# Token copies on one engine as 32-bit words, and a re-timed norm: one change to a fused group-norm and channel-attention kernel

## The reference

```python
g = x.reshape(B, 32, 6, H, W)                      # group norm: 32 groups of 6 channels
xn = (g - mean) / sqrt(var + 1e-5)
q, k, v = split(xn_tokens @ w_qkv)                 # 8 heads of 24 channels
q, k = q / |q|, k / |k| * temperature              # norms over all 2304 pixels
attn = softmax(k^T q)                              # 24 x 24 per head: attention over channels
out = x + from_tokens(attention(v, attn) @ w_out + b_out)
```

## Time and profile before

| | |
|---|---|
| median of three runs | 440.52 us (440.19 to 440.92) |
| the profiled execution | 436.02 us |
| its span, first to last instruction | 434.2 us |
| TensorE matmuls busy | 349.3 us, 80% |
| VectorE busy | 315.4 us, 73% |
| ScalarE busy | 247.4 us, 57% |
| GpSimd busy | 141.1 us, 33% |
| mean granted TensorE clock | 0.976 of full speed |
| DMA | 67.90 MB, 156 GB/s over the span |

### The profile page before, as it was taken

One profiled execution on the slowest core, in us unless ns is written; L12 is line 12 of the kernel. 1 busy time (PEld: TensorE's weight loads), 2 busy tenths in 40 slices (PEclk: granted clock), 3 DMA queues, 4 the chain that ended last, 5 costly groups with the idle time before them and its releaser, 6 DMA issues.

```text
span 434.2 us, 9296 instructions
## 1 busy us (share of the span) xinstructions
PE 349.3 (80%) x3724; PEld 238.5 (55%) x3724; DVE 315.4 (73%) x757; ACT 247.4 (57%) x360; POOL 141.1 (33%) x92
## 2 busy tenths in 40 slices
PE   0123863799988998899979997999799988996686
PEld 0022643585657565765667565756575657663443
DVE  4789932898589867897689758975897675446564
ACT  1072747881887368944986297719782788310200
POOL 0056425610571048302750075106710572001000
PEclk9999998799999999999999999999999999998699
DMA  8999300001894169605980399129921650053165
GB/s 296 286 298 249 74 2 0 2 2 75 253 324 118 53 191 323 200 2 153 335 276 3 127 283 327 30 79 292 302 95 72 194 154 20 33 188 109 51 195 190
DMA packets 30682, 67.90 MB, mean 156 GB/s; under 512 B 5360, under 2 KB 11824, under 8 KB 30640
## 3 DMA queue, kind: packets, MB, share of 16 engines
q1 hardware_dynamic: 30352, 66.86, 48.9%
q10 hardware_dynamic: 288, 0.46, 0.3%
HBM read 29.55 MB, written 28.31 MB: 133 GB/s over the span
## 4 chain that ended last, share of the span: by engine, by line
PE 32%; ACT 20%; DVE 19%; issue 16%; POOL 8%; DMA 2%; SPq 1%; POOLq 0%; ACTq 0%; DVEq 0%
PE u_ps L876 14%; ACT h_sb L481 8%; PE g_ps L876 8%; POOL l_sb L422 6%; ACT xn L475 5%; PE s_ps L876 4%; ACT tok L499 3%; DVE rk L721 3%; DVE bnst L643 3%; POOL r L434 2%; DMA x_sb<-in_x_dram 2%; DVE xn L672 2%; ACT mh L521 2%; DVE lz L731 2%; SPq L345 1%
## 5 line engine op out<-in xcount | busy, mean ns | idle before, releaser
L422 POOL TENSOR_TENSOR l_sb<-xn,h_sb 128x768 f16<-128x768 f32 x72 | 121.3, 1692 | 77.7 <-ACT h_sb L481 70.9
L800 DVE SCALAR_TENSOR_TENSOR x_sb<-u_ps,bias,x_sb 128x384 f32<-128x384 f32 x144 | 85.5, 614 | 45.5 <-PE u_ps L876 45.3
L876 PE MATMUL g_ps<-tok 128*128 128x64 f16 (+1 forms) x864 | 88.9, 242 | 29.3 <-DVE tok L702 17.1
L499 ACT COPY tok<-u_ps 128x768 f16<-128x768 f16 x104 | 78.6, 804 | 19.7 <-PE u_ps L925 19.5
L876 PEld LDWEIGHTS g_ps<-tok 128*128 128x128 f16 x864 | 58.1, 100 | 55.4 <-DVE tok L702 19.0
L481 ACT ACTIVATE h_sb<-x_sb,rb 128x768 f16<-128x768 f32 x72 | 72.6, 1017 | 20.3 <-DVE rb L695 20.3
L876 PE MATMUL u_ps<-h_sb,ml 128*128 128x384 f16 (+1 forms) x336 | 74.7, 330 | 0.0
L643 DVE BATCH_NORM_STATS2 bnst<-x_sb 128x6 f32<-128x512 f32 (+1 forms) x120 | 68.0, 624 | 7.1 <-DMA x_sb<-in_x_dram 6.9
L475 ACT ACTIVATE xn<-x_sb,rb 128x768 f32<-128x768 f32 x63 | 64.0, 1017 | 12.2 <-POOL l_sb L422 8.4
L922 PE MATMUL u_ps<-id,h_sb 128*128 128x128 f16 x288 | 49.9, 227 | 18.5 <-POOL l_sb L422 14.9
L428 POOL TENSOR_TENSOR grs<-gvar,minus_half 128x3 f32<-128x3 f32 x8 | 6.8, 852 | 135.6 <-DVE gvar L686 135.6
(11 more groups left out here) (142 smaller groups left out, 586.9 us busy)
## 6 DMA issues: line engine op xcount, KB each, us to landing
x_sb<-in_x_dram SPq DMA_DIRECT2D x48, 384.0 KB, 5.0
out_dram<-x_sb SPq DMA_DIRECT2D x48, 384.0 KB, 3.0
x_sb<-in_x_dram SPq DMA_DIRECT2D x48, 192.0 KB, 5.5
out_dram<-x_sb SPq DMA_DIRECT2D x48, 192.0 KB, 3.0
hl<-h_sb SPq DMA_DIRECT2D x48, 96.0 KB, 2.7
hl<-l_sb SPq DMA_DIRECT2D x48, 96.0 KB, 2.5
h_sb<-in_groups_dram ACTq DMA_DIRECT2D x1, 384.0 KB, 4.4
w<-in_L_conv_w_qkv_dram SPq DMA_DIRECT2D x1, 288.0 KB
```

What stands on the lines that cost most here:

```text
L422: nc.gpsimd.tensor_tensor(l_sb[:, par, t, cols], xn[:, c % XN_RING, :], h_sb[:, par, t, cols], ALU.subtract).then_inc(l_ok, 1)
L499: nc.scalar.copy(tok[:, j % TOK_RING, :, :].rearrange("p b n -> p (b n)"), slot_ps(j)).then_inc(tok_a, 1)
L800: V.scalar_tensor_tensor(out=xs, in0=block_ps(n), scalar=bias[:, t:t + 1], in1=xs, op0=ALU.add, op1=ALU.add).then_inc(out_ok, 1)
L876: return nc.tensor.matmul(dst, lhs, rhs, start=start, stop=stop, skip_group_check=True)
```

## The change

All 18 slots are copied by ScalarE, and the same bytes are read and written as 384 words of fp32 in place of 768 fp16 numbers. VectorE's copies and their semaphore are gone. The steps are placed anew. In the steady tables `sums` goes from result 4 to result 2, `var` and `scale` from 4 and 6 to 2 and 3, `v` on TensorE from slot 8 to 9, `exp` from slot 5 to 8. In step -1 `low` goes behind z8, with `bn` pieces between the chunks, and `sums`, `var` and `scale` of pair 1 stand behind the end of the Gram matrix. The `z` transposes of pair 0 wait for the group sums to be read, since both lie in one bank.

```diff
-PE_A = {2: ["flip"], 8: ["v"], 13: ["m"]}
-PE_B = {0: ["gram"], 4: ["w0", "sums"], 6: ["w1"], 12: ["scores"]}
-ACT_A = {0: ["h6"], 3: ["x7", "x8", "h7"], 5: ["exp"], 8: ["h8"], 10: ["v"], 15: ["m"]}
-ACT_B = ["t0", "t1", "t2", 0, 1, 2, 3, 4, 5, "x6"]
-POOL_B = ["power", 0, 1, 2, 3, 4, "norms", 5, 6, 7, 8]
-VEC_A = {1: ["spread"], 3: ["soft_in"], 4: ["soft_out"], 12: ["v"], 17: ["m"]}
-VEC_B = {0: ["gram", "stats"], 4: ["z", "var"], 6: ["t0", "t1", "scale", "t2"], 15: ["norms"]}
-FIRST_PE_A = {16: ["sums"]}
-FIRST_PE_B = {0: ["gram"], 2: ["w0"], 7: ["w1", "scores"]}
+PE_A = {2: ["flip"], 9: ["v"], 13: ["m"]}
+PE_B = {0: ["gram"], 2: ["sums"], 4: ["w0"], 6: ["w1"], 12: ["scores"]}
+ACT_A = {0: ["h6"], 1: ["h7"], 2: ["x8", "h8"], 8: ["exp"], 11: ["v"], 15: ["m"]}
+ACT_B = ["x0", "t0", "t1", "t2", "h0", 1, 2, 3, 4, 5, "x6", "x7"]
+POOL_B = ["power", 0, 1, 2, 3, 4, 5, "norms", 6, 7, 8]
+VEC_A = {2: ["spread", "soft_in"], 4: ["soft_out"], 12: ["v"], 17: ["m"]}
+VEC_B = {0: ["gram", "stats"], 2: ["var"], 3: ["scale"], 4: ["z"], 6: ["t0", "t1", "t2"], 15: ["norms"]}
+FIRST_PE_A = {}
+FIRST_PE_B = {0: ["gram", "sums"], 2: ["w0"], 7: ["w1", "scores"]}
-FIRST_ACT_B = [0, "t0", "t1", "t2", 1, 2, 3, 4, 5, "x6"]
+FIRST_ACT_B = [0, "t0", "t1", "t2", 1, 2, 3, 4, 5, "x6", "x7"]
-FIRST_VEC_A = {"start": ["z0", "z1", "z2", "high", "z3", "z4", "low", "bn"], 1: ["z5"], 2: ["z6"], 3: ["z7"], 4:
-               ["bn", "bn", "bn", "bn", "z8", "bn", "bn", "bn", "bn", "bn", "bn", "bn", "bn", "bn", "bn"], 13:
-               ["stats"], 16: ["var"], 17: ["scale"]}
-FIRST_VEC_B = {0: ["gram", "z", "t0", "t1"], 1: ["t2", "norms"]}
-BN_A = {6: 1, 8: 3, 9: 1, 10: 1, 13: 2, 15: 2, 16: 1, 17: 4}
+FIRST_VEC_A = {"start": ["z0", "z1", "z2", "high", "z3", "bn", "bn", "z4", "bn", "bn", "z5", "bn", "bn", "z6", "bn", "bn", "z7",
+                         "bn", "bn", "z8", "low", "bn", "bn", "bn", "bn", "bn"], 17: ["stats"]}
+FIRST_VEC_B = {0: ["gram", "var", "scale", "z", "t0", "t1"], 1: ["t2", "norms"]}
+BN_A = {6: 1, 8: 3, 9: 1, 10: 1, 13: 2, 14: 1, 15: 2, 16: 1, 17: 3}
-VECTOR_SLOTS = (1, 2, 3, 14, 16)
...
+        def slot_words(j):
+            return u_ps[:, j % RING, 0:384]
...
-                nc.scalar.copy(tok[:, j % TOK_RING, :, :].rearrange("p b n -> p (b n)"), slot_ps(j)
+                nc.scalar.copy(tok[:, j % TOK_RING, :, :].rearrange("p b n -> p (b n)").bitcast(F32), slot_words(j)
                                ).then_inc(tok_a, 1)
...
+                if q == 0:
+                    pe.wait_ge(gstep, GVAR + 1)
```

More of the change, by code:

```diff
@@ L103 @@
 SUMS_AT = next(n for n, what in PE_B.items() if "sums" in what)
-def slot_is_vector(j):
-    return j in VECTOR_SLOTS
 def preact_attention(nc, x, w_qkv, temperature, w_out, b_out, ident, groups, headmask, out):
@@ L126, in preact_attention @@
     NO = len(OUTS)
-    NV = sum(slot_is_vector(j) for j in range(SLOTS))
-    NA = SLOTS - NV
     CHUNKS = [(t, g) for g in range(GROUPS) for t in (0, 2, 1)]
@@ L253, in preact_attention @@
         tok_a = sem("tok_a")
-        tok_v = sem("tok_v")
         gram_mm = sem("gram_mm")
@@ L484, in split @@
             def split(q, par, what):
-                if isinstance(what, int) and CHUNKS[what][0] == 0 and what // 3 < GROUPS - 1:
-                    need(act, out_mm, (q - 2) * NO + (what // 3 + 1) * NO // GROUPS)
+                t, g = CHUNKS[int(str(what)[-1])]
+                if str(what)[0] != "x" and t == 0:
+                    need(act, out_mm, (q - 2) * NO + (g + 1) * NO // GROUPS)
                 if not isinstance(what, str) or what[0] == "x":
@@ L553, in step @@
                 for j in (["start"] if first else []) + list(range(SLOTS)):
-                    if j != "start" and gram and not slot_is_vector(j):
+                    if j != "start" and gram:
                         to_tok(p + 1, j)
@@ L696, in scale_shift @@
                                                op0=ALU.mult, op1=ALU.mult))
[L698 to L703, removed]
             def norms(q):
@@ L846, in step @@
                 for j in range(SLOTS):
-                    if gram and slot_is_vector(j):
-                        to_tok(p + 1, j)
                     for what in hooks(p, FIRST_VEC_A, VEC_A, LAST_VEC_A, PAIRS - 1).get(j, ()):
@@ L900, in in_tok @@
             def in_tok(q, j):
[L902 to L906, removed]
+                pe.wait_ge(tok_a, q * SLOTS + j + 1)
             def transposes(q, par, j):
```

## The result

Slower, where I had forecast faster: the kernel after takes 441.95 us (median of 20 runs, 440.21 to 444.30), the kernel before on the same chips 440.74 us (20 runs, 436.43 to 445.58). The ratio is 1.0067, with an interval of 1.0046 to 1.0088, so some 2 to 4 us. It counts only runs within 1.5% of the fastest of their kernel, which leaves out the longest runs of before and none of after; the medians of all runs are 1.2 us apart. The time is inside my range, on the wrong side of no change. The profiled execution took 442.70 us (span 440.9), and the one of before, whose rows stand above, 436.02 (span 434.2).

The account below looks back on a forecast made before the run. TensorE was taken as the bound: no gap in part B, 3.6 us of gaps in part A, and a 7.08 us stand in the head. Head -6.0, part A -6.5, part B +9.8 made -2.7: 437.8 us, range 431.0 to 443.0.

Parts of the forecast that it names:

- The copy: ScalarE's token copy as 384 fp32 words takes 0.48 us instead of 0.804; bounds 0.40 and 0.80.
- Part A: Part of a steady step from the first transposes: gains 1.09 us, bounds 0.4 and 1.5, in six steps.
- The walk: Part A followed slot by slot: slot 2 about 3.7, slot 3 near 5.95, v at 11.7, m at 15.9 us.
- Its inputs come 1.0 earlier: Softmax in part A: inputs 1.0 us earlier, flip at 4.53, so soft_in, taking 2.44, is ready at 7.5.
- Part B: From the end of slot 17: TensorE waits at sums for stats and result 1, losing 1.63 us in six steps.
- Rival (a): TensorE doesn't stand at sums in part B: -12.5 us in all, 428.0; chance 0.13.
- The head: Before the steady steps: w0 starts at 53.4 instead of 60.13; 6.0 us won, bounds 4 and 9.
- The sum: Whole kernel: -6.0 - 6.5 + 9.8 = -2.7 us, from 440.5 to 437.8.
- rival (b): ScalarE's queue becomes the bound of part A and eats its gain: +3.8 us, 444.3; chance 0.19.
- Rival (c): The word copy is no faster than 0.80, so part A loses about 0.9: +9 us, 449.7; chance 0.04.
- Rival (d): The head wins only 4 us, the rest as forecast: -0.7, no change to be told; chance 0.12.
- My 0.22 for slower: Whole kernel: the chance given to a slower result, beside 0.65 for faster and 0.13 for same.

Follow-up runs that it names:

- e2: The kernel after with the product rk computed by GpSimd instead of VectorE, sums left at result 2: 435.60 us, ratio to before 0.9947.
- e6: The kernel after with rk kept on VectorE, as four one-column products with the temperature as scalar operand: 435.22 us, ratio 0.9898.
- e1: The kernel after with sums back behind result 4, and var, scale and x0, which follow it: 428.75 us, ratio to before 0.9779.
- e5: The kernel after with sums one result later, behind result 3, and var and scale there too: 438.85 us, ratio 0.9979.
- e10: The kernel before, unchanged, run and profiled again: 440.48 us, span 438.7.
- e11: The kernel after, unchanged, profiled once more: 442.51 us, span 440.7.
- e9: The kernel before, unchanged, run and profiled again: 440.83 us, span 439.0.

## Why the prediction was wrong

**The copy: right.** The group holds 144 copies as predicted, at 479 ns for the 480 taken from the cast:

```profile
L491 ACT COPY tok<-u_ps 128x384 f32<-128x384 f32 x144 | 64.8, 479 | 27.1 <-PE u_ps L904 26.8
```

**Part A: wrong, and this is the step that failed.** "Part A gains 1.09 us" measured 0.18 (21.66 less 21.48). The walk is right up to the softmax. In us behind the first transposes (168.62), slot 2 was forecast at 3.7 and came at 3.67, slot 3 at 5.95 and came at 5.87. The sentence that failed is "Its inputs come 1.0 earlier", with `soft_in` ready at 7.5, which puts `lg` at 5.06. `lg` starts at 176.12, or 7.50. The walk started `soft_in` from `flip` on TensorE and passed over `rk`, the last instruction of `spread`, which stands ahead of it on VectorE. At its old 1.20 us it would not have mattered; it took 4.32, beside a GpSimd queue that the change rearranged. `lg` is 2.4 us late by this. Since `exp` was forecast to wait for copy 8 in any case, 0.9 of it is left behind: `v` starts at 12.64 against 11.7, and the part ends at 21.48 against 20.57. e2 and e6 give it back (part A 20.45 and 20.46). I had seen GpSimd as the source of chunks alone, and in the head as what blocks z, not as what blocks VectorE in part A.

**Part B: right.** Forecast 1.63 lost, with the gap ending when VectorE has `stats` and result 1. The gap is 1.56 and the part 1.73 longer. (2.64, 1.71 and 0.62 add up to 4.97, not to 4.89; the 0.08 then added for the signal, for which no row stands, makes the difference.) e1 and e5 show that it follows the place of `sums`. Rival (a), no stall, is refuted.

**The head: right in the cause, and my sum used a favourable clock.** `w0` was forecast at 53.4 and came at 53.52. (GpSimd's last low part was forecast at 44.3, where 33.65 + 5 x 2.1 is 44.15; a chunk cost 2.2, and it came at 44.86.) Of the 6.6 us won at `w0`, 3.8 are left at T0 of pair 1 (71.21 against 75.03), and 3.2 behind its last Gram matmul. The rest goes with the granted clock, 0.62 against 1.00: in e5, which has the same head and a clock of 1.00 there, T0 is at 69.71. Against e10, the ordinary execution, 7.8 are left at T0 and 7.1 behind that part A; e11 against e10 has 5.6 and 5.1. The 6.0 of the sum lies within what executions differ by. The part A of pair 1 itself became 0.66 longer (24.17 against 23.51), with a gap of 2.46 on TensorE, where it had been 1.41, behind copy 0, ahead of which x7 now stands; I had 0.5.

**The sum** over the profiled executions: -3.2 in the head, 6 x (1.73 - 0.18) = +9.3, and 0.6 at the end, together the 6.7 of the spans. Against e10 it is -7.1 + 9.3, which is 2.2 for the head and the steps, where the spans differ by 2.2 and the runs by 1 to 4. With the forecast 1.09 in part A in place of 0.18 it would have been -3.3, near my -2.7.

**The rivals.** The time lies between "no change" and rival (b), which I had at 444.3. Its price was near, since it too took part A's gain away and left part B's loss bare. Its mechanism was not: e2 keeps every copy in ScalarE's queue and has the gain. Rival (c), a copy no faster, is refuted by the group of 144. Rival (d), a head worth only 4, is what the two first profiles seem to say; e10 and the other profiles say that the first one of before had the fastest head of five. My 0.22 for slower was too small because all of it hung on ScalarE, while an unseen wait in a third engine would bring the same loss.

**What I had said would refute me** was an absent gap at `sums` or a step under 45.8. Neither came, so both were tests of part B; a bound on the step from above (it was forecast at 46.4 and is 47.36) was missing.

## What to carry to other kernels

When a change lets one engine feed another sooner, list what the fed engine then does in a row, and look for small instructions of other engines that already take far longer than their like beside such rows. Their time is a wait, so it may not be carried over as a duration. Move a step that waits on several results only to where its last input is ready; being early bought nothing here, on an engine with no other gap. And take two or three profiles of a kernel before a forecast that rests on less than 2% of its time, if there is a stage whose clock isn't full.

## What the hardware showed that I had not expected

- A VectorE product of 96 x 4 numbers with both inputs in SBUF outlasted one (1.20 us), two (2.72) or all three (4.32) of GpSimd's back-to-back chunks of 1.6 us, though each time it began about 0.5 us into the first. All three cases repeat from step to step of their kernel, but the first `rk` of the kernel after took 1.18 beside a row of four chunks, and 2.72 came once in e9, beside a row of two, where 1.20 is the rule. By the lock of "SBUF — State Buffer" in the Trainium skill alone (section "Terms"), which lasts one instruction, the wait would end with the chunk that is running, at about 1.2; the row of 4.32 goes beyond it, and the measurement decides. What lets `rk` in at one boundary and not at the next is open. Four products of one column with a scalar operand took 0.56 beside the same chunks. A VectorE instruction with one SBUF tensor of 96 x 2 numbers took 1.63 beside a chunk and 0.15 behind it.
- ScalarE moves 128 x 768 fp16 numbers from PSUM in 804 ns, and the same bytes as 384 words in 479.
- Between two executions of one kernel the granted clock of a short stretch of the head was 1.00 or 0.65, which was worth 1.5 us from `w0` to `w1`; by T0 of pair 1 the two stood 4.0 us apart, not all of it from this stretch. What makes it fall in one execution and not in another is open; nothing was tried on it.
